# A mixture-of-experts stage: combine weights spread by DMA and multiplied on GpSimd instead of spread by TensorE and multiplied on VectorE

## The reference, cut to what matters

```python
shared_out = silu(x_flat @ shared_gate) * (x_flat @ shared_up) @ shared_down      # H = 64
probs = softmax(x_flat @ router)                                                  # E = 8 experts
topk_scores, topk_idx = top_k(probs, 2)
combine = zeros((n, E)).at[arange(n)[:, None], topk_idx].set(topk_scores)
gate = silu(einsum('nd,edh->enh', x_flat, W_gate))
up   = einsum('nd,edh->enh', x_flat, W_up)
y    = einsum('enh,ehd->end', gate * up, W_down)
out  = shared_out + einsum('ne,end->nd', combine, y)
```

## Time and profile before

| | us |
|---|---|
| median of three runs | 450.92 |
| profiled execution | 448.98 |
| its span, first to last instruction | 446.8 |
| stage of the change, TensorE's first matmul to the next stage's | 104.17 to 220.94 |
| block ahead of it, TensorE's first matmul | 92.66 |

### The profile page before, as it was taken

One profiled execution on the slowest core, in us unless ns is written; L12 is line 12 of the kernel. 1 busy time (PEld: TensorE's weight loads), 2 busy tenths in 40 slices (PEclk: granted clock), 3 DMA queues, 4 the chain that ended last, 5 costly groups with the idle time before them and its releaser, 6 DMA issues. The chain is left out here.

```text
span 446.8 us, 6657 instructions
## 1 busy us (share of the span) xinstructions
PE 373.4 (84%) x2125; PEld 315.9 (71%) x2125; DVE 305.2 (68%) x949; ACT 154.1 (34%) x324; POOL 127.8 (29%) x141
## 2 busy tenths in 40 slices
PE   5955949968999999998756999999789796699880
PEld 5955949947888887887445899999779762693330
DVE  5846884885555566569656576876574969259997
ACT  2221154434333333332214455475465530240000
POOL 5750143006500000002000366010116567005773
PEclk9999555558999999999856599999999976699996
DMA  8930510005700000000011011111001011772335
GB/s 182 278 119 12 164 43 1 1 0 203 292 1 0 0 1 0 0 0 0 2 28 43 10 35 35 34 35 35 1 1 55 13 41 48 256 264 82 95 99 147
DMA packets 22890, 29.66 MB, mean 66 GB/s; under 512 B 4104, under 2 KB 18249, under 8 KB 22606
## 3 DMA queue, kind: packets, MB, share of 16 engines
q1 hardware_dynamic: 18350, 22.47, 17.1%
q0 software_dynamic: 1728, 3.54, 2.6%
q10 hardware_dynamic: 2784, 3.29, 2.1%
HBM read 13.48 MB, written 12.78 MB: 59 GB/s over the span
## 5 line engine op out<-in xcount | busy, mean ns | idle before, releaser
L158 POOL TENSOR_TENSOR rstd<-sm,neg_half 128x9 f32<-128x9 f32 x10 | 18.0, 1804 | 203.3 <-DVE sm L152 203.3
L807 PE MATMUL ps<-wide,gu_w 128*128 (+1 forms) x108 | 51.9, 481 | 2.2 <-PEq L704 2.2
L879 ACT ACTIVATE s<-ps 128x384 f32<-128x384 f32 (+1 forms) x60 | 29.5, 492 | 67.4 <-PE ps L811 67.0
L1767 PE MATMUL ps<-V,wide 128*128 128x129 f32 x400 | 51.3, 276 | 0.0
L838 PE MATMUL ps<-h,wd 128*128 128x384 f32 x120 | 49.8, 497 | 1.6 <-DVE h L923 1.2
L1767 PEld LDWEIGHTS ps<-V,wide 128*128 128x128 f32 x400 | 48.4, 192 | 0.1
L918 DVE TENSOR_TENSOR t<-ps,s 128x384 f32<-128x384 f32 x48 | 26.8, 557 | 30.3 <-ACT s L879 30.0
L1811 PE MATMUL ps<-ew,xTd 128*128 128x512 f32 x72 | 38.2, 669 | 3.6 <-DVE R L1480 3.5
L1480 DVE SCALAR_TENSOR_TENSOR R<-ps,dense_w,R 128x128 f32<-128x128 f32 x144 | 38.3, 343 | 1.3 <-PE ps L1811 1.1
L1232 DVE TENSOR_REDUCE mx<-ps 128x1 f32<-128x576 f32 (+1 forms) x40 | 29.8, 749 | 12.8 <-PE ps L1735 12.7
L811 PE MATMUL ps<-wide,gu_w 128*128 (+1 forms) x108 | 37.0, 343 | 0.3 <-DVE t L918 0.3
(11 more groups left out here) (252 smaller groups left out, 810.8 us busy)
## 6 DMA issues: line engine op xcount, KB each, us to landing
slots<-zrow SPq DMA_DIRECT2D x7, 768.0 KB, 7.7
xe<-slots SPq DMA_DIRECT2D x16, 192.0 KB, 4.0
slots<-wide ACTq DMA_DIRECT2D x16, 192.0 KB, 2.9
xall<-in_x SPq DMA_DIRECT2D x8, 288.0 KB, 6.1
out<-R SPq DMA_DIRECT2D x9, 192.0 KB, 2.1
Q<-sQK SPq DMA_DIRECT2D x8, 144.0 KB, 2.4
K<-sQK SPq DMA_DIRECT2D x8, 144.0 KB, 2.5
ew<-in_ew SPq DMA_DIRECT2D x1, 1024.0 KB, 5.4
```

Of the source, the lines that this page charges most:

```text
L807: nc.tensor.matmul(o, gu_w[0][:, w], xTH[:, at], start=True, stop=False)
L879: nc.scalar.activation(s4[q][:r], bank[q][:r, :CH], ACT.Silu).then_inc(s_ok[q], 1)
L1767: last = nc.tensor.matmul(bank[6 + k // 3][:, k % 3 * (C + 1):(k % 3 + 1) * (C + 1)], PT[n % 2][:, jk, i0:i0 + P], V[n % 2][:, jk, :], sta ...
```

## The change

- The matrix `sel`, its matmul and the low part of the weights are gone. The transposed weights stay in one fp32 array [8, 4608]. SyncE stores it to memory in two pieces (`combine_w`), and loads it back spread over the partitions: one call of `spread` per chunk, two DMAs of 64 partitions x 4 x 384 values each (768 KB a chunk), into one of two buffers that lie in tiles of the next stage.
- Both stores and the spreads of chunks 0 and 1 stand in the block ahead of the stage, which ends once the second store has landed.
- The product weights * silu(gate) moves from VectorE to GpSimd, 48 times. The clearing of buffers moves between those products, one memset behind each from the tenth pair on, the zero row behind the ninth.
- The writing of zeros is put between the later spreads on SyncE's queue: four DMAs behind the spread of chunk 4, one each behind those of chunks 8 to 10.
- Three PSUM banks instead of two hold up products, three buffers instead of two hold `h4`, and `down` stands three units behind the products (`LAG`).
- All loops are unrolled.

```diff
+        cB = [pt_tiles[0][:, 0:E2 // 2, 0:CH], pt_tiles[1][:, 0:E2 // 2, P:P + CH]]
+        def spread(sp, c):
+            at = slice(CH * c, CH * (c + 1))
+            by_half = combine_w[:, at].rearrange("(k two) n -> two k n", two=2)
+            for half in range(2):
+                sp.dma_start(cB[c % 2][H2 * half:H2 * (half + 1)],
+                             by_half[half:half + 1].to_broadcast([H2, E2 // 2, CH])).then_inc(cin[c % 2], 16)
...
-                for b in range(NT // TB):
-                    dve.wait_ge(cH3, b + 1)
-                    at = slice(b * TB * P, (b + 1) * TB * P)
-                    nc.vector.tensor_tensor(cT[32:32 + E2, at], bank[b % 8][:E2, :], cT[0:E2, at].bitcast(F32),
-                                            ALU.subtract).then_inc(cL3, 1)
+            @block.sync
+            def _(sp):
+                for j, (first, end) in enumerate(((0, EARLY), (EARLY, NT // TB))):
+                    at = slice(first * TB * P, end * TB * P)
+                    sp.wait_ge(cH3, end)
+                    sp.dma_start(combine_w[:, at], cT[:, at]).then_inc(cs[j], 16)
+                    if j == 0:
+                        sp.wait_ge(cs[0], 16)
+                        for c in range(2):
+                            spread(sp, c)
+                sp.wait_ge(cs[1], 16)
...
+                for u in range(UNITS):
+                    if shared(u):
+                        continue
+                    v, c = pair(u), u // NB2
+                    pool.wait_ge(cin[c % 2], 32 * (c // 2 + 1))
+                    pool.wait_ge(s_ok, u + 1)
+                    if v >= 2:
+                        pool.wait_ge(h_ok, pair_unit(v - 2) + 1)
+                    nc.gpsimd.tensor_tensor(t4[v % 2][:], cB[c % 2][:, u % NB2, :], s4[u % 2], ALU.mult).then_inc(t_ok, 1)
+                    if v == 8:
+                        nc.gpsimd.memset(zrow[:], 0.0).then_inc(z4, 1)
+                    elif v > 8 and v - 9 < len(firsts):
+                        ap, value = firsts[v - 9]
+                        pool.wait_ge(t_ok, v + 1)
+                        z.did(nc.gpsimd.memset(ap.bitcast(F32), value))
+                        z.wait()
                 for g in range(BEFORE):
                     pool.wait_ge(var5, g + 1)
                     norm_rstd(GT, g, P, rs5)
...
+                for c in range(4, CHUNKS):
+                    sp.wait_ge(t_ok, (NB2 - 1) * (c - 1))
+                    spread(sp, c)
+                    for k in range(4 * (c - 4), min(4 * (c - 3), SLOTS // (SR * 12))):
+                        sp.dma_start(slots[k * SR * 12:(k + 1) * SR * 12, :].rearrange("(p t) c -> p t c", t=12),
+                                     zrow[:SR]).then_inc(zf4, 16)
...
+                def feed(u):
+                    c, k = divmod(u, NB2)
+                    tokens = slice(CH * c, CH * (c + 1))
+                    if u >= 2:
+                        pe.wait_ge(s_ok, u - 1)
+                        if shared(u - 2):
+                            pe.wait_ge(h_ok, u - 1)
+                    product3(bank[u % 2][:, :CH], slice(2 * k * P, (2 * k + 1) * P), tokens).then_inc(g_ps, 1)
+                    if not shared(u):
+                        v = pair(u)
+                        if v >= 3:
+                            pe.wait_ge(h_ok, pair_unit(v - 3) + 1)
+                        product3(bank[2 + v % 3][:, :CH], slice((2 * k + 1) * P, (2 * k + 2) * P), tokens).then_inc(u_ps, 1)
...
+                for u in range(UNITS + LAG):
+                    if u < UNITS:
+                        feed(u)
+                    if u >= LAG:
+                        down(u - LAG)
...
+                def silu(u):
+                    act.wait_ge(g_ps, u + 1)
+                    if u >= 2:
+                        if shared(u - 2):
+                            act.wait_ge(h_ok, u - 1)
+                        else:
+                            act.wait_ge(t_ok, pair(u - 2) + 1)
...
+                def hidden(u):
+                    if u >= 3:
+                        dve.wait_ge(dn, u - 2)
...
+                        dve.wait_ge(u_ps, pair(u) + 1)
+                        dve.wait_ge(t_ok, pair(u) + 1)
+                        nc.vector.tensor_tensor(h4[u % 3][:], bank[2 + pair(u) % 3][:, :CH], t4[pair(u) % 2][:],
+                                                ALU.mult).then_inc(h_ok, 1)
```

More of the change, by code:

```diff
@@ L852, in trip @@
-                def trip(i, first, final):
-                    for u in range(UB):
-                        if u + 1 < UB:
-                            feed(i, u + 1)
-                        elif not final:
-                            feed(i + 1, 0)
-                        down(i, u)
-                        if u == 1 and not first:
-                            back(i - 1, 1)
-                        if u == NB2 + 1:
-                            back(i, 0)
-                pe.wait_ge(wz3, 1)
@@ new lines, in down, with back @@
+                def down(u):
+                    c, k = divmod(u, NB2)
+                    o, q = bank[5 + c % 2][:, :CH], u % 3
+                    if k == 0 and c >= 2:
+                        pe.wait_ge(yS, c - 1)
+                    pe.wait_ge(h_ok, u + 1)
+                    nc.tensor.matmul(o, wd[:, k, :], h4[q][:], start=k == 0, stop=k == NB2 - 1).then_inc(dn, 1)
+                def back(c):
+                    pe.wait_ge(yS, c + 1)
+                    if c:
+                        pe.wait_ge(R_ok, c)
+                    for t in range(3):
+                        last = nc.tensor.transpose(bank[7][:, t * P:(t + 1) * P], y4[c % 2][:, t * P:(t + 1) * P], ident)
+                    last.then_inc(zt, 1)
@@ new lines, in channels @@
+                def channels(c):
+                    act.wait_ge(dn, NB2 * (c + 1))
+                    if c >= 2:
+                        act.wait_ge(zt, c - 1)
+                    nc.scalar.activation(y4[c % 2], bank[5 + c % 2][:, :CH], ACT.Copy).then_inc(yS, 1)
+                silu(0)
+                for u in range(UNITS + LAG + 1):
+                    if u + 1 < UNITS:
+                        silu(u + 1)
+                    c, k = divmod(u - LAG + 1, NB2)
+                    if k == 0 and c >= 1:
+                        channels(c - 1)
@@ L953, in _ @@
                 f = Steps(dve, dve5)
[L954 to L960 removed]
+                for u in range(UNITS + LAG + 2):
+                    if u < UNITS:
+                        hidden(u)
+                    c, k = divmod(u - LAG - 2, NB2)
+                    if k == 0 and c >= 1:
+                        residual(c - 1)
+                    if UNITS - 2 * NB2 <= u < UNITS:
+                        if u == UNITS - 2 * NB2:
+                            dve.wait_ge(R_ok, CHUNKS // 2)
+                        ahead(u - UNITS + 2 * NB2)
+                residual(CHUNKS - 1)
         local.close()
```

180 lines of the change are left out of this document (46 added, 134 removed).

## The result

The changed kernel takes **448.09 us** (median of 20 runs, 446.28 to 451.78), the kernel before beside it 451.7 (20 runs, 449.1 to 455.01). The ratio is **0.993, 95% interval 0.990 to 0.995**: 3.2 us less, between 2.1 and 4.4; the medians themselves are 3.6 apart. Predicted were 446.5, and 3.6 us less.

A forecast was written before the change was run, and what follows sets the result against it. TensorE's stream was taken to bound the stage. Matmul -8.4, lag -2.9, start +5.3 and end +2.4 gave -3.6 us: 445.4 from the profiled execution, 447.3 from the median, middle 446.5; 80% range 441.5 to 453.

The forecast's parts named there:

- TensorE's beat: Middle of the stage: dropping the spreading matmul saves 8.4 us, the longer lag 2.9; a chunk takes 8.30 us.
- GpSimd's product: Middle of the stage: the product takes 1.03 us on GpSimd and costs nothing, hidden behind TensorE's stream.
- Rival B: Middle of the stage: GpSimd becomes the bound, products waiting through VectorE's instructions; 454.6 to 456.5 us, chance 0.12.
- The memsets: Between GpSimd's products: in twelve pairs a memset of 0.63 us follows, 1.86 us a pair, still hidden.
- The start: Block ahead of the stage: waiting for the second store delays TensorE's first matmul to 109.5, +5.3 us.
- The rate: Start of the stage: spreads of 64 partitions move at 228 GB/s, so two chunks take 6.9 us.
- yes, it waits its turn: Start of the stage: the second store is held up behind the four spreads on the same DMA queue.
- Rival A: Start costs little: spreads at 128-partition rate or store not queued behind them; +1.3 to +2.0 us, chance 0.24.
- The end: End of the stage: VectorE's normalisation waits for GpSimd's inverse root behind the last product, +2.4 us.
- The sum: Whole kernel: -8.4 - 2.9 + 5.3 + 2.4 = -3.6 us, giving 446.5 us.
- Rival C: Later spreads: slow zeros delay chunk 5's spread by 4 us, half absorbed; +2, about 448.5 us, chance 0.08.
- D: TensorE's work is not saved because longer waiting ahead of the stage drops it to half clock; chance 0.06.

The follow-up runs named there:

- again: The changed kernel rerun without any edit for a second profiled execution: 448.85 us, 0.994 of the kernel before.
- root earlier: Changed kernel with GpSimd's first inverse root put behind the product of unit 53 instead of behind all 48: 447.78 us, 0.988 of the kernel before.
- product on VectorE: Changed kernel with the weights * silu(gate) product back on VectorE, GpSimd keeping its memsets: 447.66 us, 0.989 of the kernel before.
- product twice: Changed kernel with GpSimd making each of the 48 products twice, first into an unread spare tile: 474.84 us, 1.055 of the kernel before.
- store ahead of chunk 1: Changed kernel with the second store issued between the spreads of chunks 0 and 1: 445.89 us, 0.985 of the kernel before.
- wait moved: Changed kernel with SyncE's wait for the second store moved from the block's end to ahead of chunk 2's spread: 440.35 us, 0.974 of the kernel before.
- store from ScalarE: Changed kernel with the second store issued on ScalarE's DMA queue instead of behind the spreads on SyncE's: 446.8 us, 0.989 of the kernel before.
- halves: Changed kernel with spreads of chunks 0 and 1 split: lower 64 partitions from SyncE's queue, upper from ScalarE's: 446.13 us, 0.994 of the kernel before.
- long: Changed kernel with even chunks' spreads in contiguous runs of 6144 bytes instead of 1536: 448.63 us, 0.996 of the kernel before.
- rows: Changed kernel with four same-shaped DMAs from 256 different input rows ahead of the first spreads: one run, 459.06 us beside 452.86 of the kernel before.

## Why the prediction was nearly right

**TensorE's beat.** Predicted 8.30 us a chunk, measured 8.26: the spreading matmul and the shared unit's wait went as worked out. A pair unit takes 139.11 - 137.43 = 1.68 us for 1.87 before, and with 0.35 for the transposes 1.19 is left for the shared unit, which took 1.41. Twelve chunks give 12 x 0.98 = -11.8 us, predicted -11.3.

**GpSimd's product.** Predicted 1.03 us, measured 1.009; nothing of it reaches TensorE in the middle. Rival B is out: no product waited through VectorE's instructions (the 48 take 1.000 to 1.027 us). The doubled product shows that this was the cover and not luck. The memsets were undercounted, 27 and the zero row for the twelve of the sum, and this too stayed under the cover.

**The start.** Predicted 109.5 (+5.3). In the five profiles in which the block ahead is untouched (changed, again, root earlier, product on VectorE, product twice) it is 109.76 to 111.59, mean 110.4: +6.3. The spreads were issued when the sum had it (99.37 to 99.56 for 99.5); from there to the first matmul it took 10.2 to 12.1 us, mean 11.0, where the sum had 10.0. The rate was nearly right (206 to 221 GB/s for 228 in the stretch from 104 to 107); in the profile of 111.59 it was lower at either side of it, 188 and 151. **The step that failed is the reason for the store's lateness, "yes, it waits its turn"** behind the spreads on the same queue: on another queue it came no sooner, its packets moving only when the spreads had nearly gone, and with half the bytes ahead the stage began 3.5 us sooner. It was right in size only because the spreads' bytes are the same in both readings. Rival A, on the rate and on the queue, is out.

**The end.** Predicted +2.4 through the root behind the products. The three waits came where they were named, and the 10.5 from the start of unit 57 to the last down product was 215.49 - 205.39 = 10.1. Taking the root forward gave 2.9 back at the end, 1.8 of it for the waits and 1.1 for the clock. So the waits were less than the 2.4, and the size came out near with help that I had not foreseen: after the wait TensorE falls to its half clock, and from the last down product to the next stage it takes 4.05 us instead of 2.96. The idle time shown, 2.19 + 0.32 + 0.19 = 2.7 us, is no measure of the cost: a down product that follows a wait takes 0.91 and more, where in a row they follow at 0.65. The clock fell in four profiles with these waits (changed, again, store ahead of chunk 1, wait moved: 9.31 or 9.32 us in the stretch) and not in four others (store from ScalarE, halves, long, rows: 8.22 or 8.23).

**The sum.** The stage's length fell by 8.8 to 8.9 us, predicted 8.9; of the 11.8 that the chunks gave, 3.0 were given back, nearly all of it at the end: 1.8 for the waits behind the root and 1.1 for the clock. The start took 6.3, so the stage alone says -2.6; the ratio says -3.2 and the medians -3.6. The terms were off by -0.5 (chunks), +1.0 (start) and +0.5 (end), so that the medians came out at just the -3.6 is partly luck. The time itself, 448.09 for 446.5, is off because the kernel before measured 451.7 beside it, where the sum had started from 450.92 and 448.98. Rival C did not show (GpSimd waited 1.4 us in all for spreads), nor D at the start: there the half clock lasts 3.7 us, from 111.59 to 115.25, and 3.3 before. The half clock that did cost time came at the end, which D had not named.

**What I left out** is what the profile said plainly: the wait at the block's end was the dearest term of the sum, and nothing in the stage needed that store before chunk 5.

## What to carry to other kernels

A wait at the end of a block holds every engine: put it on the one that issues the reader, and price the bytes already under way ahead of a small transfer, here also from another queue. Work moved to an idle engine is free only while its beat stays below the bound engine's, and it is paid where that engine's next duty stands behind it. Compare traces by the marks of the stage: executions of one kernel spread over more (446.28 to 451.78) than the change was worth.

## What the runs showed of the hardware that was not expected

- A store of 80 KB, issued from another queue behind 1.57 MB of loads, moves only when they have nearly gone (no packet of it in the 5 us after its issue; 7.4 us from issue to the stage's start, where 8 KB alone take 2.3).
- Loads of 64 partitions move some 206 to 244 GB/s with full DMA engines, in runs of 1536 or 6144 bytes, from one row or many. Two queues with such loads were served mostly one after the other.
- GpSimd's 384-column product with both inputs in SBUF takes 1.009 us, though VectorE works beside it; no waiting through VectorE's instructions shows.
- TensorE fell to half its clock after a wait of 2.2 us in the changed kernel, and not after the same wait of 2.19 in "store from ScalarE". What tells the two apart stays open.
